# Folding centroids into the merged feed-forward matrices: one 576-column merge ahead of the routing dots, in place of two separate products

## The reference, cut to what matters

```python
def _L1_cond_ref(x, weight, adapter_ids):
    w = weight[adapter_ids]                      # one of 8 matrices for each sample
    return jnp.einsum('bsi,boi->bso', x, w)

def _L1_ffn_ref(input, weight, bias, centroids, assignments):
    dots = softmax(x @ centroids.T / 0.1)        # x: output of the adapter; 64 centroids
    hits = dots > 0.01
    query_sel = jnp.any(hits, axis=1)            # for each row
    cluster_sel = jnp.any(hits, axis=0)          # over ALL rows, for each centroid
    row_sel = cluster_sel[assignments]
    dense = x @ weight.T + bias
    return jnp.where(query_sel[:, None] & row_sel[None, :], dense, 0)

x = x + _L1_ffn_ref(_L1_cond_ref(x, L1_cond_weight, ids), ...)
```

## Time and profile before

| | |
|---|---|
| median of 3 runs | 808.13 us (807.05 to 809.34) |
| profiled execution, span | 807.1 us; its time is not listed apart from the span |
| PE busy | 744.9 us (92%), DVE 49%, ACT 26%, POOL 36% |
| granted TensorE clock, mean | 0.971 of full |
| chain that ended last | PE 82%, POOL 6%, DVE 5%, issue 3%, DMA 2% |
| L1571 merges / L1586 dots / L1533 centroid products in that chain | 11% / 4% / 3% |

### The profile page before, as it was taken

How to read it: one execution, slowest core, us unless ns; L and a number is a source line. 1 busy time by engine, 2 the same in 40 slices (tenths; PEclk the granted TensorE clock), 3 DMA queues, 4 the chain that set the end, 5 groups by cost and what they waited for, 6 DMA issues and landing times.

```text
span 807.1 us, 12472 instructions
## 1 busy us (share of the span) xinstructions
PE 744.9 (92%) x3672; PEld 579.4 (72%) x3673; DVE 394.0 (49%) x815; ACT 210.7 (26%) x364; POOL 288.0 (36%) x308
## 2 busy tenths in 40 slices
PE   2278989999999999999999899999999998999995
PEld 1266767768777677777776664588888876888884
DVE  6854674334243243432433230366666754666664
ACT  3232312222213132221221111344444421121110
POOL 4242451452614525335154130000000003777776
PEclk9689999999999999999999899999999979999998
DMA  9447006420512214114101008354444331544441
GB/s 196 154 113 261 1 19 191 118 92 1 156 53 66 90 52 156 52 38 118 52 0 53 0 1 312 115 168 143 134 126 142 92 104 47 162 143 149 167 151 39
DMA packets 61920, 85.34 MB, mean 106 GB/s; under 512 B 14098, under 2 KB 30834, under 8 KB 60866
## 3 DMA queue, kind: packets, MB, share of 16 engines
q1 hardware_dynamic: 57618, 68.17, 28.8%
q0 software_dynamic: 4272, 16.78, 5.1%
HBM read 67.99 MB, written 18.78 MB: 108 GB/s over the span
## 4 chain that ended last, share of the span: by engine, by line
PE 82%; POOL 6%; DVE 5%; issue 3%; DMA 2%; ACT 1%; SPq 0%; POOLq 0%; ACTq 0%; DVEq 0%
PE acc L1446 22%; PE acc L1571 11%; PE acc L1429 11%; PE work L1402 8%; PE acc L1639 6%; PE bcast L1586 4%; PE work L1551 4%; PE work L1533 3%; PE bcast L1439 3%; PE work L1412 3%; PE bcast L1639 3%; POOL out_tile L701 2%; POOL out_dram L704 2%; PE work L1392 2%; PE bcast L1540 1%
## 5 line engine op out<-in xcount | busy, mean ns | idle before, releaser
L625 POOL TENSOR_TENSOR gatedT_lo<-gated,gatedT_hi 128x512 fp32r<-128x512 f32 x64 | 82.4, 1292 | 115.9 <-ACT gatedT_hi L780 115.9
L1446 PE MATMUL acc<-lora_b_hi,gatedT_hi 128*128 128x512 f32 x256 | 107.9, 421 | 5.2 <-POOL gatedT_lo L625 4.9
L1446 PE MATMUL acc<-lora_b_hi,gatedT_lo 128*128 128x512 f32 x256 | 101.0, 395 | 0.0
L1446 PE MATMUL acc<-lora_b_lo,gatedT_hi 128*128 128x512 f32 x256 | 100.7, 393 | 0.0
L1121 DVE TENSOR_TENSOR gated<-bcast,res_hidden 128x512 f32<-128x512 f32 x64 | 43.5, 690 | 115.6 <-PE bcast L1439 115.4
L614 POOL TENSOR_TENSOR yT_lo<-y_masked,yT_hi 128x512 fp32r<-128x512 f32 x32 | 41.2, 1289 | 118.4 <-ACT yT_hi L767 118.2
L780 ACT ACTIVATE gatedT_hi<-gated 128x512 fp32r<-128x512 f32 x64 | 40.2, 633 | 154.3 <-DVE gated L1121 154.3
L847 ACT ACTIVATE x1T_hi<-work 128x512 fp32r<-128x512 f32 x79 | 47.2, 598 | 113.1 <-PE work L1551 98.4
L1402 PE MATMUL work<-uT_hi,hankel 128*128 128x512 f32 (+3 forms) x256 | 66.2, 332 | 4.1 <-DMA hankel<-k_rev 2.4
L1446 PEld LDWEIGHTS acc<-lora_b_hi,gatedT_hi 128*128 128x128 f32 x256 | 48.5, 190 | 26.7 <-POOL gatedT_lo L625 10.5
L693 POOL COPY out_row_of_tile<-slot_out_row 128x1 uint32 (+1 forms) x40 | 7.3, 183 | 153.3 <-PE acc L1571 147.6
(11 more groups left out here) (252 smaller groups left out, 1422.9 us busy)
## 6 DMA issues: line engine op xcount, KB each, us to landing
hankel<-k_rev SPq DMA_DIRECT2D x32, 512.0 KB, 9.0
dots_rows<-x_sorted SPq DMA_DIRECT2D x52, 256.0 KB, 2.7
cond_w<-in_L_cond_weight_dram SPq DMA_DIRECT2D x32, 256.0 KB, 3.0
cond_w<-x_sorted SPq DMA_DIRECT2D x27, 256.0 KB
x_group<-in_x_dram SPq DMA_DIRECT2D x24, 256.0 KB, 4.4
cond_w_raw<-in_L_cond_weight_dram SPq DMA_DIRECT2D x6, 1024.0 KB, 6.3
setup<-in_L_ffn_B_dram SPq DMA_DIRECT2D x4, 512.0 KB, 7.4
cond_w<-in_L_cond_weight_dram SPq DMA_DIRECT2D x2, 1024.0 KB, 6.4
```

The costliest lines, as they stand in the source:

```text
L625: g.tensor_tensor(gT[j % 2][1][:, :], g32[j % 2][:, :], gT[j % 2][0][:, :].bitcast(F32), ALU.subtract).then_inc(g_lo, 1)
L1446: last = mm(acc[i][:, :], gT[j % 2][a][:, P * i:P * i + P], bw[b][:, j, :], start=False, stop=(j == NP - 1 and a == 1))
```

## The change

`merged_w` and `merged_c` become one tensor `mwc`, for each adapter, block and part (hi, lo) two halves of 288 columns: 256 of the feed-forward matrix and 32 of the centroids. The separate centroid products, with their tensors, loads and semaphores, are gone. A merge block now is 24 matmuls of 288 columns into a pair of PSUM banks; there are two pairs, so block k waits for the low part of block k - 2. The centroids are split hi and lo as the feed-forward weights are (one DVE subtraction more in the set-up).

All 32 merge blocks now run first, one after another, and then eight steps of dots alone. PE waits for the last merged low part ahead of the first transpose. Dots have two sets of PSUM banks (`dotb`) and rows are loaded five tiles ahead. The first adapter's splits moved into layer 0's last group: on ACT ahead of the routing's exponential, on DVE behind the routing. Row selection comes after the second output tile instead of ahead of the first.

```diff
+WIDE = 2 * (L // 2 + C // 2)
+HALF = WIDE // 2
...
-        mw = [alloc(l1, f"merged_w_{n}", [P, IDS, LB, L], F32R) for n in ("hi", "lo")]
-        mc = alloc(l1, "merged_c", [P, IDS, LB, 2 * C], F32R)
+        mwc = alloc(l1, "merged_w_and_c", [P, IDS, LB, 2, 2, HALF], F32R)
...
-        acc = [bank(f"acc{i}") for i in range(GH)]
+        accp = [ctx.enter_context(nc.psum_tensor(f"acc{j}", [P, 2, 512], F32)) for j in range(GH // 2)]
+        acc = [accp[i // 2][:, i % 2, :] for i in range(GH)]
...
+        db = acc[2:] + acc[:2] + [t[:, :] for t in bb]
+        dotb = [[t[:, :] for t in bb], acc[:2]]
...
@@ scalar, group @@
+                if last:
+                    for k in range(LB):
+                        split_high(0, k)
                 act.wait_ge(r_sub, gr + 1)
...
@@ scalar @@
+            for n in range(XB):
+                act.wait_ge(x1_st[n], 16 * len(range(n, NG, XB)))
+            with act.Fori(0, IDS - 1) as e:
                 for k in range(LB):
                     merged_high(e, k)
                     split_high(e + 1, k)
...
+            def dots_step(st, n, first):
+                for w in range(TD):
+                    x_high(TD * st + w, (n + w) % 2, xd_ps, xd_hi)
+                    if w == 2 and not first:
+                        dots_exp(st - 1)
...
@@ vector @@
+            with dve.Fori(0, IDS - 1) as e:
                 for k in range(LB):
                     merged_low(e, k)
                     split_low(e + 1, k)
...
+            def dots_step(st, n, first):
+                for w in range(TD):
+                    x_low(TD * st + w, (n + w) % 2, xd_hi, xd_lo)
+                    if not first:
+                        dots_part(st - 1, 1 - n, w)
...
@@ tensor @@
             def merge(e, k):
                 pe.wait_ge(cw_lo, LB * e + k + 1)
...
-                    pe.wait_ge(m_lo, LB * e + k - 3)
+                    pe.wait_ge(m_lo, LB * e + k - 1)
                 steps = [(a, b, o) for a, b in ((0, 0), (0, 1), (1, 0)) for o in range(LB)]
                 for s in steps:
                     a, b, o = s
-                    m = mm(acc[k][:, :], w_sp[a][:, o, P * k:P * k + P], f_w[b][:, o, :],
-                           start=s == steps[0], stop=s == steps[-1])
+                    for h in range(2):
+                        m = mm(accp[k % 2][:, h, 0:HALF], w_sp[a][:, o, P * k:P * k + P], wf[b][:, o, h, :],
+                               start=s == steps[0], stop=s == steps[-1])
...
+            def dots_step(st, n, last=False):
                 for w in range(TD):
+                    if w + 1 < TD:
+                        transpose_tile(st, w + 1, n)
+                    elif last:
+                        transpose_first()
+                    else:
+                        transpose_tile(st + 1, 0, 1 - n)
+                    dots_tile(st, w, n)
...
+            pe.wait_ge(m_lo, LB * IDS)
+            transpose_tile(0, 0, 0)
...
+            for n in range(RB):
+                dense_tile(n, n, 1)
+                if n == 1:
+                    row_select()
```

More of the change, by code:

```diff
@@ L225, in build @@
         query = alloc(fold, "query_sel", [P, NTD])
[L226 to L229, removed]
         fold.close()
-        rows = [w_id[:, n, :] for n in range(LB)] + [t[:, :] for t in rows2]
+        rows = [t[:, :] for t in rows2] + [w_id[:, n, :] for n in range(LB)]
         outt = [alloc(l1, f"out_tile_{n}", [P, L])[:, :] for n in range(RB)]
@@ L471, in _ @@
             hankels(NG - 1)
[L473 to L487, removed]
+            with sp.Fori(0, IDS - 1) as e:
+                for k in range(LB):
+                    sp.wait_ge(cw_lo, LB * e + k + 1)
+                    load_block(e + 1, k)
             for n in range(XB):
@@ L497, in load_rows @@
                              ).then_inc(s, 16)
[L499 to L526, removed]
+            for w in range(TD):
+                if w == 2:
+                    sp.wait_ge(cw_lo, LB * IDS)
+                load_rows(w, rows[w], s_rl[w])
+            with sp.Fori(1, IDS) as st:
+                for w in range(TD):
+                    sp.wait_ge(xd_ps, TD * st + w - TD + 1)
+                    load_rows(TD * st + w, rows[w], s_rl[w])
             for n in range(RB):
+                if n < TD:
+                    sp.wait_ge(xd_ps, NTD - TD + n + 1)
                 load_rows(n, rows[n], s_rl[n])
@@ L815, in _ @@
             group(NG - 1, True)
[L817 to L842, removed]
             def x_high(t, n, ps, hi):
@@ L1172, in group @@
                 routing(gr)
+                if last:
+                    for k in range(LB):
+                        split_low(0, k)
                 if not last:
@@ L1578, in dots_tile, with transpose_tile @@
+            with pe.Fori(1, IDS) as e:
+                for k in range(LB):
+                    merge(e, k)
+            def transpose_tile(st, w, n):
+                pe.wait_ge(xd_lo, TD * st + w + 1)
+                pe.wait_ge(s_rl[w], 16 * (st + 1))
+                transpose_rows(rows[w], (n + w) % 2).then_inc(xd_ps, 1)
+            def dots_tile(st, w, n):
+                t = TD * st + w
                 pe.wait_ge(xd_lo, t + 3)
                 if w == 0:
-                    pe.wait_ge(dt_ev, 2 * e + 2)
+                    pe.wait_ge(dt_ev, 2 * st + 2)
@@ L1607, in _ @@
-            e = IDS - 1
-            for w in range(TD):
-                if w < TD - 1:
-                    transpose_next(TD * e + w, TD + w + 1, TD * (IDS // 2 - 1))
-                if w == 0:
-                    merge(e, 0)
-                dots_tile(e, w, 1)
-            for k in range(1, LB):
-                merge(e, k)
-            pe.wait_ge(s_dn, DOTS * IDS + 1)
-            pe.wait_ge(s_l1c, 3)
-            mm(bb[0][0:C, 0:P], hitany[:, :], ones[:, :], start=True, stop=True).then_inc(cnt_ps, 1)
```

264 lines of the change are left out of this document (110 added, 154 removed).

## The result

| | before | after |
|---|---|---|
| median, us | 808.13 (807.05 to 809.34) | 836.59 (835.08 to 837.06, 4 runs) |
| ratio | | 1.034 [1.0325, 1.0356] |
| profiled execution: span | 807.1 | 832.1 (its time 835.08; the other three spans 833.8 to 834.3) |

The change made the kernel 3.4% slower; 835 us was forecast, in a range of 812 to 846. First the page of the kernel after: engine totals, the strip of TensorE's granted clock in 40 slices, and the chain by line.

What follows compares the result with a forecast made beforehand. PE was taken as the bound (92% busy). Layer 0's end to first output matmul goes from 189.2 to 212.9 us, +23.7; with 0.5 + 2.4 + 1.0, +27.6 on 807.1; span 1.0 below median: 835 us, range 812 to 846.

Steps and rivals of the forecast that it cites:

- rival A: Dots stage: clock falls at the entry, stays at 0.50 to the output tiles; 835 us, range 825 to 847; 76%.
- merges, 768 x 0.135: Layer 1 merge blocks: 768 matmuls of 288 columns at an interpolated 0.135 us each, 103.7 us.
- wait for the last scatter: Start of merges: first merged high part waits for layer 0's last scatter, so PE waits; +1.6 us.
- entry to the first dots: Last merge to first dots, now bare: 4.8 us at full clock, about 5.1 at half.
- dots, 39 tiles: Dots stage after the merges: PE-bound at clock 0.50, 2.6 us a tile, 101.4 us.
- first two tiles at full clock: Start of the dots stage: first two tiles may still run at full clock, -1.5 us.
- last group of layer 0, four splits moved in: Splits ahead of the exponential delay the routing chain by 1.0 us; 0.5 us charged.
- row selection, third output tile: Row selection moved behind output tile 1: its product, waits and the delayed third tile add 2.4 us.
- half-speed outputs: First output matmuls: about 5 us at clock 0.50 where it was 2.9, +1.0 us.
- B: Dots stage: clock holds at 1.00, 1.86 us a tile, 803 us, faster than before; 12%.
- C: Dots stage: clock now up, now down, half of the tiles at either level, 819 us; 9%.
- D: Merges: the pair of half matmuls costs what 384 columns do, merges 138 us, total 869 us; 3%.

Runs made afterwards that it cites:

- e1: Changed kernel plus two unread 512-column matmuls for each tile of dots and 21 at the entry to the dots: 809.76 us, ratio 1.0013.
- e7: e4 with the first transposes moved ahead of the wait for the last low part and 8 unread matmuls between: 798.49 us, ratio 0.9872.
- e2: Changed kernel plus the 21 unread matmuls at the entry to the dots alone, none in the steps: 834.3 us, ratio 1.0309.
- e5: e4 without the unread matmul for each tile; early read and entry matmuls stay: 802.32 and 799.11 us, but 826.09 and 826.21 in two other runs.
- e6: e4 without the early read of the adapter number; all unread matmuls stay: 810.89 and 811.23 us, but 841.29 and 841.48 in two other runs.
- e3: Changed kernel with PE reading the tile's adapter number ahead of its wait for x1T_lo, nothing else: 831.97 us, ratio 1.0289.
- e4: Changed kernel with the adapter number read early, one unread matmul for each tile and 21 at the entry: 800.19 us, ratio 0.9880.

## Why the prediction was right

The time (836.59 against 835), its sign and its cause were as forecast: rival A, the dots at half speed from the entry to the output tiles. e1 shows the cause rather than argues it: the same order with the clock held is at 1.0013, so the clock makes the 3.4%. Step by step, from the profiled run:

| step | forecast | measured |
|---|---|---|
| merges, 768 x 0.135 | 103.7 | 102.4 (block 3.20, matmul 0.133) |
| wait for the last scatter | 1.6 | 1.46 (one block start 4.66 behind the last, not 3.20) |
| entry to the first dots | 5.1, at half clock (4.8 at full) | 5.07, all at full clock |
| dots, 39 tiles | 101.4 (2.6 each) | 99.6 (2.553 each) |
| last dots and transposes | 2.6 | 2.48 |
| first two tiles at full clock | -1.5 | 0: none was |
| **interval, against 189.2** | **212.9** | **210.9** |
| last group of layer 0, four splits moved in | +0.5 | 0 |
| row selection, third output tile | +2.4 | +2.0 (5.24 against 3.22) |
| half-speed outputs | +1.0 | +0.3 (first period 4.93 against 4.61) |
| fourth output tile waits for DVE | not seen | +2.0 |
| POOL one step late at the end (why stays open) | not seen | +1.2 |
| time outside the span | 1.0 | 2.5 to 3.0 in four runs |

*Right, by the rows.* 288 columns were read off as 0.135, near the 256 row, and came at 0.133; reading in 32-column pieces costs nothing that shows (a tile's dots take 620.98 - 620.17 = 0.81 us in e7, as before). That transposes and dots alone hold TensorE at 0.50 once it has fallen was read from 4.5 us of before, and held for 102 us. The Trainium skill ("TensorE: Matmul & The Clock Gate", "Why this matters for your kernels") warns of long idle gaps between matmul bursts. By that alone the gaps here would pass: the longest wait of PE at the entry was 2.14 us, and in e2 it was 0.98 us in the dots ahead of the fall at 605.28. The clock fell at both places, so the traces do not agree that short gaps are safe, as the prediction had weighed it. The row that it weighed against a fall, 38 to 46 us at 1.00, was cut too short: in the same trace, of the kernel before, the clock is at 0.50 from 47.41 to 54.24, so the row says little for B.

*Mis-sized, and why.* The last group's splits delay ACT's exponential, by 0.5 us where 1.0 was forecast: it starts 441.93 - 438.74 = 3.2 us behind logitsT, where it was 441.10 - 438.38 = 2.7, and the four copies take 2.18 us in a row, not 4 x 0.62. But PE reaches the gates 12.70 us behind logitsT and reached them 12.69 before, by these rows of the timeline of before; the earlier trace rows had only the exponential:

```profile
438.38 0.59 ACT L772 ACTIVATE logitsT<-work 16x512 f32<-16x512 f32 x1 [7.23 <-PE work L1412]
...
451.07 0.73 PE L1439 MATMUL bcast<-combineT,expert_selection 32*128 32x512 f32 x2
```

PE works through its base matmuls until then, so the delay was hidden, and the charge of 0.5 should have been nothing. The fourth output tile is a true miss of the method: I followed the row selection only to the tile behind which it stands. But DVE, which waits for the selection until 701.48, then has the post-processing of two finished tiles in its queue, and the low part of the fourth tile's rows stands behind that (705.54). Whatever is held up should be followed to what is queued behind it on its engine.

*Luck.* The entry came at 5.07 us with 5.1 in the sum, but at full clock, for which the forecast had 4.8. Errors of both signs cancel: +2.0 and +1.2 not seen and 1.5 to 2 outside the span, against -2.0 in the interval, -0.5 for the splits, -0.4 and -0.7 at the outputs. Layer 0 ended 2.5 us earlier in the profiled run, though the change adds there: before had a half-speed stretch at 453.60 to 460.42, and this run had none. It comes and goes between profiled runs whose layer 0 is the same (e7 had it, e1 did not), and the other three runs of after have spans 1.7 to 2.2 us longer.

*Rivals.* B had the right kind of stage, but not its size: at full clock a tile takes 1.95 (e1, with two fillers), not 1.86. Its 803 is besides a span, 807.1 - 3.9, without the 1.0 us outside it that the forecast of 835 has: 804 as a time. With the delays at the outputs that gives an estimate of 804 + 3.6 + 3.2 = 811, no gain. The mechanism for which it asked, PE at 1.00 ten tiles in, did not occur in the profiled run of this change. C and D are out: one fall and one rise, and 0.133 for a half. The "3.16 us each" of the output tiles is 3.20 by the trace of before; it stands on both sides of the comparison and changes nothing.

## What to carry to other kernels

Before work is regrouped by kind, ask of each new stage on its own how thick its stream on TensorE is: small matmuls may cost double once the large ones between them are gone (transposes and dots of a tile: 0.41 + 0.9 us before, 2.55 after), and taking out 35.75 us of products cost 57 us elsewhere (35.75 + 21.7). If a stage has to be thin, an unread matmul for each step can be cheaper than the lost clock (101 of them gave back 26 us here), and a register load belongs ahead of the semaphore wait, not behind it. Judge such a stage from several runs: two kernels here came out at either of two times.

## What the runs showed of the hardware that was not expected

- More work was less time: 101 extra matmuls took the kernel from a ratio of 1.034 to 1.0013, at the same order of everything else.
- One program can keep the clock in one run and lose it in the next: two of four runs of e5 held it, and two of four of e6, with 25 and 30 us between the groups.
- The clock stayed at 0.50 for 105.8 us (589.54 to 695.36), with PE busy 102.00 of 102.00 us of it, and in e3 for 99 us (588.91 to 687.89), with even its weight loads busy 97.80 of 97.80 us. It rose behind the first output matmuls, which have 512 columns; that their width did it was not tested apart.
- A register load behind a wait cost 0.30 us for a tile at full clock (1.952 in e6 to 1.648 in e4) and 0.08 at half clock (2.55 to 2.47).
